# A two-layer graph network: the split of its gathered rows between PE and GpSimd by a table over the groups

## What is computed

```python
h = jnp.maximum(_layernorm(x, axis=-1), 0.0)
x = x + _L0_gnn_ref(h, edge_index, edge_weight1, edge_attr_3, edge_attr_5, L0_gnn_W)
h = jnp.maximum(_layernorm(x, axis=-1), 0.0)
x = x + _L1_gnn_ref(h, ...weights..., src, dst, edge_type_86)
```

## Time and profile before

| what | value |
| --- | --- |
| median of 3 runs | 3294.89 us (3294.35 to 3296.32) |
| the profiled execution | 3295.84 us |
| its span, first to last instruction | 3294.0 us |
| mean granted clock of PE | 0.986 of full speed |
| layer 0, first L609 to last L1062 | 62.6 to 1607.8 us |
| layer 1, first gather to last L1062 | 1630.9 to 3275.3 us |

### The profile page before, as it was taken

How to read it: one execution, slowest core, us unless ns; L and a number is a source line. 1 busy time by engine, 2 the same in 40 slices (tenths; PEclk the granted TensorE clock), 3 DMA queues, 4 the chain that set the end, 5 groups by cost and what they waited for, 6 DMA issues and landing times.

```text
span 3294.0 us, 108331 instructions
## 1 busy us (share of the span) xinstructions
PE 2972.4 (90%) x41934; PEld 2392.0 (73%) x41934; DVE 2602.5 (79%) x3897; ACT 895.1 (27%) x1910; POOL 2414.9 (73%) x2546
## 2 busy tenths in 40 slices
PE   2999999999999999999789999999999999899997
PEld 2777777777777777777677777777777777777776
DVE  7777777777777777777678888888888888888886
ACT  1111111111111111111344444444444444444342
POOL 6777777777777777777377777777777777777774
PEclk9999999999999999999789999999999999999998
DMA  4111111111111111111233333333333333332331
GB/s 138 28 28 28 28 28 28 27 28 27 28 27 29 27 29 27 29 27 29 67 55 58 55 59 59 57 56 59 58 57 56 59 58 58 55 58 54 58 57 40
DMA packets 220288, 150.94 MB, mean 46 GB/s; under 512 B 122954, under 2 KB 201083, under 8 KB 219901
## 3 DMA queue, kind: packets, MB, share of 16 engines
q0 software_dynamic: 81312, 41.79, 12.3%
q1 hardware_dynamic: 138013, 100.79, 12.3%
q10 hardware_dynamic: 576, 2.40, 0.2%
HBM read 136.54 MB, written 8.22 MB: 44 GB/s over the span
## 4 chain that ended last, share of the span: by engine, by line
PE 32%; POOL 9%; issue 5%; DVE 4%; DVEq 1%; DMA 0%; ACT 0%; POOLq 0%; ACTq 0%
PE ps L609 17%; POOL xg L541 9%; PE ps L634 5%; PE ps L675 4%; PE ps L622 3%; DVE scratch L960 2%; PE ps L657 1%; PE ps L572 1%; PE ps L645 1%; DVE Z L1044 0%; DMA xg<-h_table,idx 0%; DVE aggT L1062 0%; DVEq L960 0%; DVE blocks L951 0%; DVEq L1062 0%
## 5 line engine op out<-in xcount | busy, mean ns | idle before, releaser
L541 POOL DMA_INDIRECT xg<-h_table,idx x2541 | 2404.1, 946 | 844.1 <-issue 758.9
L609 PE MATMUL ps<-h,blocks 128*128 128x448 f32 x8190 | 1803.0, 372 | 237.5 <-DVE scratch L960 213.4
L609 PEld LDWEIGHTS ps<-h,blocks 128*128 128x128 f32 x8190 | 1501.3, 188 | 458.5 <-issue 324.1
L1044 DVE TENSOR_TENSOR Z<-coef,ps 128x864 f32<-128x864 f32 (+1 forms) x522 | 734.4, 1448 | 16.6 <-DVE ps L985 0.2
L951 DVE TENSOR_TENSOR blocks<-scratch,ps 128x896 fp32r<-128x896 int16 x585 | 630.1, 1077 | 34.4 <-PE ps L609 34.4
L675 PE MATMUL ps<-Z,xg 128*32 128x32 f32 (+3 forms) x25008 | 507.8, 215 | 8.3 <-DVE Z L1044 7.9
L675 PEld LDWEIGHTS ps<-Z,xg 128*32 128x32 f32 x25008 | 403.9, 110 | 93.0 <-issue 70.2
L1062 DVE TENSOR_TENSOR aggT<-aggT,ps 64x128 f32 (+1 forms) x262 | 74.1, 283 | 485.1 <-PE ps L657 478.4
L960 DVE SCALAR_TENSOR_TENSOR scratch<-ramp_sb,scratch,ps 128x448 f32<-128x448 f32 x585 | 396.7, 678 | 7.8
L830 ACT ACTIVATE p_left<-ps 96x128 f32<-96x128 f32 (+2 forms) x262 | 64.6, 246 | 1189.3 <-PE ps L645 1140.8
L965 DVE TENSOR_REDUCE xg<-scratch 128x32 f32<-128x448 f32 x585 | 362.8, 620 | 20.2
(11 more groups left out here) (105 smaller groups left out, 1109.4 us busy)
## 6 DMA issues: line engine op xcount, KB each, us to landing
xg<-h_table,idx POOLq DMA_INDIRECT x2541
rows_b<-typ_short SPq DMA_DIRECT2D x130, 258.0 KB
scratch<-q_short SPq DMA_DIRECT2D x260, 96.0 KB
rows_b<-dst_short SPq DMA_DIRECT2D x130, 126.0 KB
coef<-in_edge_dram SPq DMA_DIRECT2D x130, 54.0 KB
att_tab<-p_table SPq DMA_DIRECT2D x393, 8.1 KB
p_table<-Z SPq DMA_DIRECT2D x8, 297.0 KB, 3.9
X<-in_x_dram SPq DMA_DIRECT2D x7, 224.0 KB, 4.6
```

The source lines that it names most:

```text
L541: pool.indirect_dma_start(xg[:, g.q, t - g.s * J, :], None, h_table[n], bass.IndirectOffsetOnAxis(ap=idx[:, t:t + 1], axis=0)).then_inc(L. ...
L609: last = pe.matmul(found_ps[b], blocks[:, b, c, :], h_2[:, a, c], start=(c == 0 and a == 0), stop=(c == NCH - 1 and a == 1))
L1044: dve.tensor_tensor(Z[:, b, js, 0:C * WN].rearrange("p j (c n) -> p j c n", n=WN), coef[:, js, :].unsqueeze(3).broadcast_to([P, k, C, WN]) ...
```

## The change

- The number of tiles that PE finds is a table over the groups. Layer 0: 2 in the first 8 and the last 8 full groups, between them 3, 3, 3, 2 by turns. Layer 1: 3 in each fourth group from 8 on (8, 12, ... 116), else 2.
- In whole: 346 tiles where there were 325 in layer 0, 288 where there were 260 in layer 1; the gathers of POOL are 21 and 28 fewer.
- DVE, ACT and SP: 16 steps written out, a loop of 11 iterations over 8 steps, the rest written out. The counts that semaphores are compared with are worked out for any table (`in_loop`).
- The flag of the general passes is loaded behind step 15 of the usual pass; the branch stays behind the pass.
- `sums_done` is gone: PE waits for the last add itself.

```diff
-NP = [[3, 2, 3, 2], [2, 2, 2, 2]]
+EIGHT = 8
+LOOP = [2, FULL // EIGHT - 3]
+NP = [[2 if s < 8 or s >= FULL - 8 else [3, 3, 3, 2][s % 4] for s in range(FULL)], [3 if 8 <= s < FULL - 10 and s % 4 == 0 else 2 for s in range(FULL)]]
...
+def in_loop(count, i, r):
+
+    if isinstance(i, int):
+        return count(i * EIGHT + r)
+    at = LOOP[0] * EIGHT + r
+    return count(at) + (i - LOOP[0]) * (count(at + EIGHT) - count(at))
...
-    for t in range(4):
+    for t in range(LOOP[0] * EIGHT):
         step(0, t)
-    with eng.Fori(0, FULL // 4 - 1) as i:
-        for u in range(4):
-            step(i, 4 + u)
-    for t in range(FULL // 4 * 4, NG + lag):
+    too_far = look(eng) if isinstance(k, int) else None
+    with eng.Fori(*LOOP) as i:
+        for u in range(EIGHT):
+            step(i, u)
+    for t in range(LOOP[1] * EIGHT, NG + lag):
         step(0, t)
...
-def all_steps(body, lag):
+def all_steps(eng, body, lag, look):
 
     for s in range(NG + lag):
+        if s == LOOP[0] * EIGHT:
+            too_far = look(eng)
         body([Group(0, s - d, 0) if 0 <= s - d < NG else None for d in range(lag + 1)])
+    return too_far
...
+        def look_beyond(eng):
+
+            eng.wait_ge(beyond_set, 1)
+            return eng.value_load(beyond[0:1, 0:1], min_val=0, max_val=1)
+
         def all_passes(eng, passes, restart=None, finish=None):
 
-            passes(0)
-            eng.wait_ge(beyond_set, 1)
-            too_far = eng.value_load(beyond[0:1, 0:1], min_val=0, max_val=1)
+            too_far = passes(0)
             with eng.If(too_far):
...
             edge_sums(0)
-            pe.wait_ge(sums_done, 1)
+            pe.wait_ge(layers[0].added, NG)
...
             edge_sums(1)
-            pe.wait_ge(sums_done, 2)
+            pe.wait_ge(layers[1].added, NG)
...
-
-                dve.wait_ge(L.added, NG)
-                dve.nop().then_inc(sums_done, 1)
```

More of the change, by code:

```diff
@@ L86 @@
 assert NOWHERE < 1 << 15 and NREL <= 1 << 8
-assert NCH * MC == M and FULL % 2 == 0 and all(sum(np) % 2 == 0 for np in NP) and JT <= JH and PS <= P
+assert NCH * MC == M and FULL % 2 == 0 and all(sum(np) % 2 == 0 and len(np) == FULL for np in NP) and JT <= JH and PS <= P
 def gathers_of_pass(n, q):
-    return len(range(q, FULL, 4)) * (J - NP[n][q]) + (JT if q == FULL % 4 else 0)
+    return sum(J - np for np in NP[n][q::4]) + (JT if q == FULL % 4 else 0)
+def in_loop(count, i, r):
[3 more added lines that the diff above has]
+    return count(at) + (i - LOOP[0]) * (count(at + EIGHT) - count(at))
 class Group:
@@ L101, in __init__ @@
         self.q = r % 4
-        self.s = i * 4 + r
+        self.s = i * EIGHT + r
         self.tail = isinstance(self.s, int) and self.s == FULL
@@ L110, in order2 @@
     def order2(self):
-        return self.k * len(range(self.b, NG, 2)) + self.i * 2 + self.r // 2 + 1
-    def order4(self):
-        return self.k * len(range(self.q, NG, 4)) + self.i + self.r // 4 + 1
+        return self.k * len(range(self.b, NG, 2)) + in_loop(lambda s: s // 2 + 1, self.i, self.r)
     def halves(self):
@@ L122, in full_order2 @@
     def full_order2(self):
-        return self.k * len(range(self.b, FULL, 2)) + self.i * 2 + self.r // 2 + 1
+        return self.k * len(range(self.b, FULL, 2)) + in_loop(lambda s: s // 2 + 1, self.i, self.r)
     def gathers(self, n):
@@ L129, in gathers, with of_loop @@
             return gathers_of_pass(n, self.q)
-        return (self.i + self.r // 4 + 1) * (J - NP[n][self.q])
+        return in_loop(lambda s: sum(J - np for np in NP[n][s % 4:s + 1:4]), self.i, self.r)
+    def of_loop(self):
+        return self.s if isinstance(self.s, int) else LOOP[0] * EIGHT + self.r
     def gathered_tiles(self, n):
-        return self.nj if self.tail else J - NP[n][self.q]
+        return self.nj if self.tail else J - NP[n][self.of_loop()]
     def tiles_before(self, n, later=0):
-        r = self.r + later
-        of_pass = FULL // 4 * sum(NP[n]) + sum(NP[n][0:FULL % 4])
-        return self.k * of_pass + (self.i + r // 4) * sum(NP[n]) + sum(NP[n][0:r % 4])
+        return self.k * sum(NP[n]) + in_loop(lambda s: sum(NP[n][0:max(s, 0)]), self.i, self.r + later)
     def found_tiles(self, n):
@@ L145, in found_tiles @@
             return []
-        np = NP[n][self.q]
-        return [(NPM - np + i, J - np + i, (sum(NP[n][0:self.q]) + i) % 2, self.tiles_before(n) + i + 1) for i in range(np)]
+        at = self.of_loop()
+        np = NP[n][at]
+        return [(NPM - np + i, J - np + i, (sum(NP[n][0:at]) + i) % 2, self.tiles_before(n) + i + 1) for i in range(np)]
 def unit(u):
@@ L158, in wait, with over_steps @@
         eng.wait_ge(sem, n)
-def over_steps(eng, k, body, lag):
+def over_steps(eng, k, body, lag, look):
     def step(i, r):
-        body([Group(i, r - d, k) if not isinstance(i, int) or 0 <= i * 4 + r - d < NG else None for d in range(lag + 1)])
-    for t in range(4):
+        body([Group(i, r - d, k) if not isinstance(i, int) or 0 <= i * EIGHT + r - d < NG else None for d in range(lag + 1)])
+    for t in range(LOOP[0] * EIGHT):
         step(0, t)
-    with eng.Fori(0, FULL // 4 - 1) as i:
-        for u in range(4):
-            step(i, 4 + u)
-    for t in range(FULL // 4 * 4, NG + lag):
+    too_far = look(eng) if isinstance(k, int) else None
[3 more added lines that the diff above has]
+    for t in range(LOOP[1] * EIGHT, NG + lag):
         step(0, t)
-def all_steps(body, lag):
+    return too_far
+def all_steps(eng, body, lag, look):
     for s in range(NG + lag):
+        if s == LOOP[0] * EIGHT:
+            too_far = look(eng)
         body([Group(0, s - d, 0) if 0 <= s - d < NG else None for d in range(lag + 1)])
+    return too_far
 def build(nc, x, src_t, dst_t, dnext_t, dst, etype, edge, tile_first, tile_last, group_first, group_last, group_of_tile,
@@ L330, in build @@
         centred_turned, agg_turned = sem("centred_turned"), sem("agg_turned")
-        sums_done, x_set, out_set = sem("sums_done"), sem("x_set"), sem("out_set")
+        x_set, out_set = sem("x_set"), sem("out_set")
         p_w4_zero = sem("p_w4_zero")
@@ L501, in edge_loads @@
                     sp.wait_ge(tab_rel_set, 1)
-                all_passes(sp, lambda k: over_steps(sp, k, lambda gs: loads(gs[0]), 0))
+                all_passes(sp, lambda k: over_steps(sp, k, lambda gs: loads(gs[0]), 0, look_beyond))
             for c in range(NCH):
@@ L551, in one_pass @@
                         pool.nop().then_inc(L.recounted, 1)
+                    too_far = None
                     for s in range(NG):
+                        if s == LOOP[0] * EIGHT and isinstance(k, int):
+                            too_far = look_beyond(pool)
                         gather(Group(0, s, k))
+                    return too_far
                 all_passes(pool, one_pass)
@@ L702, in one_pass @@
                         pe.wait_ge(L.recounted, k)
[L703 to L707, removed]
+                        return over_steps(pe, k, step, 2, look_beyond)
+                    return all_steps(pe, step, 2, look_beyond)
+                all_passes(pe, one_pass, None, lambda: pe.wait_ge(L.added, (PASSES + 1) * NG))
             pe.wait_ge(weights_in, 128)
@@ L845, in one_pass @@
                         act.wait_ge(L.moved_on, k * (2 + 2 * n))
-                    over_steps(act, k, step, 2)
+                    return over_steps(act, k, step, 2, look_beyond)
                 all_passes(act, one_pass)
@@ L1116, in one_pass @@
                         dve.wait_ge(L.recounted, k)
-                    over_steps(dve, k, step, 3)
+                    return over_steps(dve, k, step, 3, look_beyond)
                 dve.wait_ge(agg_cleared, 1)
                 all_passes(dve, one_pass, restart, lambda: dve.wait_ge(L.added, (PASSES + 1) * NG))
-                dve.wait_ge(L.added, NG)
-                dve.nop().then_inc(sums_done, 1)
             dve.memset(zero[:], 0.0).then_inc(pad_zero, 1)
```

## The result

| | before | after |
| --- | --- | --- |
| median | 3295.61 us (4 runs) | 3412.81 us (3411.57 to 3415.14, 4 runs) |
| the profiled execution | 3295.84 us, span 3294.0 | 3411.57 us, span 3409.7 |

The ratio is 1.0357, 95% interval 1.0342 to 1.0372: the change costs 117 us. The forecast was 3426 us in a range of 3405 to 3460.

What follows compares the result with a forecast made beforehand. PE was taken to bound both layers, POOL only layer 1's last 40 groups. Layer 0 +61.5, layer 1 +69.4, looks 0 and loops 0 sum to +130.9 us, giving 3426 us, range 3405 to 3460.

Steps and rivals of the forecast that it cites:

- the two parts named for it: Allowances for the range's low side: 2 us from the flag's look, and 2.85 instead of 2.93 us a tile.
- A tile's price, 2.93 us: On PE, one more found tile is 14 matmuls that nothing hides, costing 2.93 us a step.
- Layer 0, +61.5 us: PE in layer 0: 21 more found tiles at 2.93 us each, +61.5 us.
- Layer 1, +69.4 us: Layer 1: 28 tiles at 2.93 us on PE, +82.0, less 12.6 us no longer lost to POOL.
- DVE's thin margin in a step of three: Layer 1: DVE readies the second half of `Z` at 2413.3 us; PE wants it 0.9 us after 2413.6.
- The looks, 0 us: The flag's load and `sums_done`: -2 us at PE's layer ends, up to +1.8 behind step 15; taken as 0.
- The loops of 8, 0 us: Back branches of the longer loops stay cheap or covered by DVE's queue: 0 us, upper end 84 us.
- the rival that rested on it: Loops of 8 stall at each turn: +11 to +42 us in layer 1, 3437 to 3510 us in all; 9%.
- POOL's lead at the ends of layer 0: POOL falls back 2.15 us a group, 17 us in eight groups, but its lead of some 26 us outlasts it.
- POOL as the bound (3234 us): POOL's queue sets the step, so 49 fewer gathers at 1.248 us give -61 us, 3234 us; 3%.
- layer 1 hiding its tiles: PE's slack in layer 1 absorbs its tiles while POOL's relief counts: -34.9 us there, 3322 us; 3%.
- DVE in the steps of three: DVE binds in layer 1's 28 steps of three, 0.5 to 2.4 us each: 3440 to 3493 us; 8%.

Runs made afterwards that it cites:

- POOL relieved: The kernel before with one gather fewer in each full group, 260 in all, and no more work for PE: 3279.22 us.
- old table: The changed kernel with the table of before, 324 tiles in layer 0 and 2 a group throughout layer 1: 3286.28 us, ratio 0.9975.
- layer 1 only: The changed kernel with the table of before in layer 0 (324 tiles) and the new one in layer 1: 3353.50 us.
- both tables by the rates: The changed kernel with 322 or 320 tiles in layer 0, and in layer 1 threes only in groups 3, 6, 9, 12: 3290.40 and 3287.55 us.
- the last three: The changed kernel with 322 tiles in layer 0; in layer 1 two late threes, none, or four late threes: 3282.10, 3284.77 and 3287.27 us.
- five tables tried after this run: The changed kernel with 322 or 320 tiles in layer 0 and early, late or no threes in layer 1: 3290.40, 3287.55, 3282.10, 3284.77, 3287.27 us.
- runs of one layer at a time: The changed kernel with the new table in layer 0 alone, then in layer 1 alone: 3347.01 and 3353.50 us.

## Why the prediction was right, point by point

**What bounds.** That PE sets both layers and POOL only the end of layer 1 held. The relief of POOL by 260 gathers gave 15.5 us of 324, and in the changed kernel POOL waits for PE's sums, as the prediction's last part said. The forecast was 13 us too high. No miss made good for another: the terms below all err on the same side. One sign did not come: PE is 91% busy, not nearer 95%, and from 800 to 1200 us 93.9% for 93.4. The forecast's own lower end, 3418 us, comes to 3420 by the two parts named for it.

**A tile's price, 2.93 us.** It measured 2.87 us in layer 0 and 2.86 in layer 1. The 2.93 came from a mean of steps set against a single short one; the short steps average 10.34, not 10.33, and the old long ones 13.26 us against 13.20 after the rewrite. That is 0.06 to 0.07 too much for each of 49 tiles, 3 us of the 13.

**Layer 0, +61.5 us.** It measured +54.0 from the span's start to the last add. 21 x 2.87 is 60.3. Off it go 65 old steps of three that are 0.06 us shorter (4 us), and 1.5 us by which PE's clock rose earlier. The prediction had costed the rewrite of the counts and loops at nothing. This term of the sum was the one missed outright, and it was a gain.

**Layer 1, +69.4 us.** It measured +62.4. DVE's thin margin in a step of three held: 15.03 us, with no wait of PE on `Z` to speak of. POOL's lateness was worth 14.0 us for 12.6, since the tail gave more than the 2.2 us of one wait: its last three steps take 19.2 us where they took 23.2, and 19.1 with POOL relieved. PE idles less there, and its clock was low from 3379.8 to 3383.2 us, where before it was low from 3260.1 to 3270.3. The smaller price of a tile is 2 us of this term's miss and the shorter steps of two are some 2; the last 1.5 us or so are not accounted for.

**The looks, 0 us.** They gained 1.0 and 0.9 us at the ends. The prediction had set the same against it in mid-pass, and there it cost nothing: the load stands at 237 us in PE's queue (below), between a step of 10.30 us, where the short ones average 10.33, and one of 13.27, where the long ones take 13.13 to 13.53. So this term was -1.9 us, the lower end of what the prediction allowed. That PE's own branch ends last, and not DVE's signal, held. The transposes of the changed kernel wait for nothing that the profile names, and start where the branch of 3.51 us, begun at 1660.8, ends:

```profile
1660.72 0.65 PE L679 MATMUL ps<-squares,p_left 48*64 48x128 f32 x2 [0.40 <-ACT p_left L851]
1664.33 2.93 PE L594 MATMUL ps<-ident,aggT 32*128 32x32 f32 x23 [2.96 <-issue]
```

```profile
L406 PEldq COMPARE_BRANCH  x2: 3509/3554/3598, 1660.8 to 3390.4; - x2
```

```profile
L401 PEldq TENSOR_LOAD <-beyond x2: 313/400/486, 237.3 to 1910.3; - x2
```

**The loops of 8, 0 us.** In the changed kernel DVE's branch takes 0.05 to 0.07 us in 22 iterations, as the earlier trace rows has it, and the sequencer goes on 0.22 to 0.27 us later each time. For this kernel the rival that rested on it falls:

```profile
L179 DVEq COMPARE_BRANCH  x22: 50/56/73, 331.7 to 3038.5; - x22
```

It does not fall for loops of this size. In the seven variants whose layer 0 has the old table or one near it (old table, layer 1 only, both tables by the rates, and the last three), DVE's queue stands still for 2.9 to 4.7 us behind each of the ten back branches in layer 1, and for 0.22 to 0.27 in layer 0. In the run with the new table in layer 1 alone, the first turn there branches at 1945.0 us, and the queue's next instruction, the first of the new iteration, starts at 1948.7; in the changed kernel 0.3 us lie between the two.

```profile
L179 DVEq COMPARE_BRANCH  x11: 55/63/73, 1945.0 to 2979.9; - x11
...
L179 DVEq FUSED_REGOPS  x10: 85/85/85, 1948.7 to 2880.4; - x10
```

The cover that the prediction named, two `Z` and an `R`, hides most of it: in that run layer 1 is 5.6 us longer than in the changed kernel, with the idle times of DVE shown above, and in the run with the old table 2.0 us longer than in the one with the new table in layer 0 alone, which is within the scatter. Only the table of layer 0 differs between such pairs, and so the code that stands ahead of the loop; why that decides was not tested. The list of DMA queues has 135 packets of instructions on its queue q14 in that run, and 86 in the changed kernel. All five tables tried after this run have the stalls, so what they show against one another stands. That the changed kernel has none of these stalls was luck as far as the prediction goes, but their size was not what the rival had: some 4 to 6 us in layer 1 where it had 11 to 42.

The Trainium skill's page "Runtime: NRT & Kernel Launch" (section "Instruction fetch mechanics") lets only branches stall whose target is outside the lines held. The traces agree with it as far as they go: 3.5 us for the skip past the general passes, 2.9 to 4.7 us and more packets of instructions for the loop of 8 in layer 1 of seven variants, and nothing for it in the changed kernel. Where the lines lie no trace shows.

**POOL's lead at the ends of layer 0.** It lasted. POOL falls back in the first eight groups, 12.48 us a group against 10.33, and has no wait on PE's sums before 315 us; from 1550 to 1662 us, where it falls back again, neither PE nor DVE waits for a gather.

**The other rivals.** POOL as the bound (3234 us) and layer 1 hiding its tiles (3322 us) fell by the runs of one layer at a time; DVE in the steps of three fell by their 15.03 us.

## What to carry to other kernels

When two engines show equal rates, look at who waits for whom, stretch by stretch. Taking work off an engine gains only where another waits for it, and putting it on one whose steps have no idle time costs its full time at once, here 2.87 us a tile for a gather of 1.25 us that nobody waited for. Between two engines joined by a few buffers the balance holds over stretches, not over the sum: relief counts where the relieved engine is late, and load put early on the slower one is paid a second time by the one that runs ahead and must stop. An engine at 73% busy can be issuing without rest: count its gaps, and what ends them.

## What the runs showed that was not expected

**PE's clock falls at waits of 2 to 3 us.** In the kernel before with 12 matmuls a tile, PE waits up to 3.1 us before the sums. The timeline has such a wait of 2.06 us at 449 us, and the matmuls behind it are slower (four of L657 in 1.12 us, where they take 0.62):

```profile
449.25 0.50 PE L675 MATMUL ps<-Z,xg 128*32 128x48 f32 x32 [2.06 <-issue]
...
449.92 0.63 PE L675 MATMUL ps<-Z,xg 128*32 128x48 f32 x32
...
451.52 0.85 PE L675 MATMUL ps<-Z,xg 128*32 128x48 f32 x32
```

The granted clock of the stretch from 450 to 457 us is 0.51, that is the lower level, 1.2 GHz, and 1.00 again from 460 us:

```profile
450.00:457.00 7.00, 6.45 (x79) 5.41 (x80) 3.79 (x6) 0.96 (x3) 5.34 (x6) 0.51 0.11 16
460.00:515.00 55.00, 48.93 (x685) 38.75 (x683) 41.97 (x63) 6.11 (x19) 41.58 (x45) 1.00 0.17 29
```

It happened 14 times between 450 and 1471 us, for 3 to 10 us each, and the mean clock of the run was 0.969 for 0.986. Each of these falls begins between 1.0 us before and 2.0 us behind the end of a wait of 1.7 to 3.1 us; five waits of 2.0 to 2.5 us have none. The kernel before has no wait of PE over 0.9 us from 200 to 1500 us, and no such fall. So an engine that is relieved until it waits can also work slower. Whether that cost this run any time is not shown, since POOL issues there without rest.

**The clock at the start differs between executions.** PE's first found tile starts at 62.3 to 62.9 us in all runs, and the granted clock rises from the lower level at 65.2 to 68.6 us. At half the clock each microsecond of that is half a microsecond of PE's work, an estimate that the run with POOL relieved bears out: its clock rose 2.7 us earlier than in the kernel before, with the same table, and its first add came 1.3 us earlier. The changed kernel's profiled execution had it 3.2 us earlier than before's, which is the 1.5 us of its difference.
